# A fused macaron block: VectorE's preparation of batch 0's attention laid out anew over rounds 1 to 12 of the first feed-forward phase

## Chip, cores and metric

The kernel runs on one core of one Trainium2 chip. The metric is device time in microseconds of one execution. The five engines (TensorE, VectorE, ScalarE, GpSimd and SyncE, which issues most transfers) run programs of their own and meet at semaphores. In the profile they are PE, DVE, ACT, POOL and SP; PEld is TensorE's weight load.

## The reference, cut to what matters

`x` has 8 batches of 1024 rows of 128 float32 values.

```python
x = x + 0.5 * ffn(layernorm(x))        # FFN 1
x = x + attn(layernorm(x))             # 4 query heads, 2 key heads, causal, width 32
x = x + 0.5 * ffn(layernorm(x))        # FFN 2

def ffn(x):                            # int weights / 127, hidden 384
    return (silu(x @ wg.T) * (x @ wu.T)) @ wd.T

def attn(x):
    h = x * rsqrt(mean(x**2) + 1e-6) * norm_w
    q, k, v = h @ Wq, h @ Wk, h @ Wv
    q, k = q / |q|, k / |k|
    p = softmax(causal(q @ k.T * exp(log_temperature)))
    return x + gate * ((p @ v) @ Wo)
```

## The kernel before

All rows stay in the chip (`X`), as 16 chunks of 512 rows (4 tiles of 128). FFN 1 runs over the chunks in rounds 0 to 15, then attention runs over the 8 batches (two chunks each), then FFN 2 over the 16 chunks. Every engine's order is written out by hand: `pipeline` calls, in each round k, a list of steps with an offset to the chunk.

In round k of FFN 1:

- VectorE (`ffn_dve`): `hidden` of chunk k (silu times up, writes `H`, L327), then whatever `between[k]` holds, `stats` of chunk k+6 (L306), `residual` of chunk k-1 (L343, waits for TensorE's down product), `aggregate` of chunk k+6 (L314). Where this text says "slot k", it means the point right behind `hidden(k)`, where `between[k]` is issued.
- ScalarE (`ffn_act`): `silu(k)` (L476), four normalising activations of chunk k+3 (L458), `x_hi(k+3)` (the float16 high part of the normalised rows, L469, shown as `w_int<-XN` since it reuses that space), `h_hi(k)` (writes `HH`, L482).
- GpSimd (`ffn_pool`): `x_lo(k+3)` (the float16 low part, L426, also shown as `w_int<-XN,w_int`), `h_lo(k)` (writes `HL`, L433), and in odd rounds the row factors of two later chunks (L400 to L405, with the power at L403). Behind rounds 9 and 10 it also splits the attention input of chunks 0 and 1 in two (`AS`, L931 and L938).
- TensorE (`ffn_pe`): gate(k+1), down(k-1), up(k+1) as groups of 6 products of 512 columns (L507) and a down group that starts with L558 and goes on with `HH` and `HL` (L569). Behind rounds 11 to 14 it also does the first projections of batch 0 (L737), which wait for the weights `QKVO` (`s_wready`) and for the turned `AS` (`AXT`).
- SyncE turns each chunk's `w_int` into `XT`, and behind chunks 13 and 14 the two `AS` into `AXT`.

Batch 0's attention needs a preparation that VectorE does between these rounds: moments of chunks 0 to 3 (`stats`, L993 to L998), the weights scaled by powers of two and split into two float16 parts (`weights_scaled`, `weights_low`), a few one-column factors (`weights_factors`), the row factors of chunks 0 and 1 by an integer seed and three Newton rounds of three operations each (`factors`, i.e. `first_factors`), and the two normalised chunks (`normalise`, L1008, four operations of 128x128 each, writes `AN`). Before the change they lie in rounds 3 to 12:

```python
{3: rows("stats", 0), 4: rows("stats", 1), 5: weights_scaled,
 6: rows("factors", 0), 7: rows("factors", 1),
 8: weights_and_rows, 9: rows("normalise", 0, (2, 4)),
 10: rows("normalise", 1), 11: factors_and_rows, 12: rows("stats", 3),
```

Chunk 0 cannot be taken up by `stats` before its residual is added, which is in round 1.

Of the kernel before, what the change touches and what calls it, by code (L numbers as in the profile page):

```python
# [5 lines left out]
ALU = mybir.AluOpType  # L6
# [4 lines left out]
def macaron_kernel(nc, x, norm_w, wq, wk, wv, wo, gate, log_temp, w_gate, w_up, w_down, out):  # L11
# [38 lines left out]
    with ctx:  # L50
        def sb(name, shape, d=f32):
            return ctx.enter_context(nc.sbuf_tensor(name, shape, d))

        def sem(name):
            return ctx.enter_context(nc.semaphore(name))
# [17 lines left out]
        qkvo = sb("qkvo", [P, DQ + 2 * DK + D])  # L73
        QKVO = sb("QKVO", [P, 2, DQ + 2 * DK + D], f16)
# [5 lines left out]
        ipw = sb("ipw", [P, 4])  # L80
# [7 lines left out]
        k_lim = sb("k_lim", [P, 1])  # L88
# [30 lines left out]
        FV, FT = [sb(n, [P, 2, 2, TPC]) for n in ("FV", "FT")]  # L119
# [53 lines left out]
        a_xh0, a_fac = sem("a_xh0"), sem("a_fac")  # L173
# [808 lines left out]
        def att_dve(e, shift, first=None):  # L982
# [47 lines left out]
                e.tensor_scalar(SS[half][:, :, :], SS[half][:, :, :], 1.0 / (QSCALE * QSCALE), k_lim[:, 0:1],  # L1030
                                ALU.mult, ALU.max).then_inc(a_ss, 1)

            def root(done, n, S2, Y, T, rounds=(0, 3)):

                if rounds[0] == 0:
                    e.tensor_scalar(Y.bitcast(i32), S2.bitcast(i32), -0.5, float(0x5f3759df), ALU.mult,
                                    ALU.add).then_inc(done, 1)
                for r in range(*rounds):
                    e.wait_ge(done, n + 3 * r + 1)
                    e.scalar_tensor_tensor(T, Y, -0.5, S2, ALU.mult, ALU.mult).then_inc(done, 1)  # L1040
                    e.wait_ge(done, n + 3 * r + 2)
                    e.tensor_tensor(T, T, Y, ALU.mult).then_inc(done, 1)
                    e.wait_ge(done, n + 3 * r + 3)
                    e.scalar_tensor_tensor(Y, T, 1.5, Y, ALU.add, ALU.mult).then_inc(done, 1)
# [6 lines left out]
            def first_factors(part):  # L1051

                var, mean = AMV4[:, 0:2, :, 1], AMV4[:, 0:2, :, 0]
                V1, Y = [XP[:, 16 * i:16 * i + 16].rearrange("p (a m t) -> p a m t", a=2, m=2)
                         for i in range(2)]
                if part == 0:
                    e.wait_ge(a_stat, 4)
                    e.wait_ge(s_wtl, 3)
                    e.tensor_scalar(V1[:, 0, :, :], var, LN_EPS, None, ALU.add).then_inc(a_fac, 1)
                    e.wait_ge(a_fac, 1)  # L1060
                    e.tensor_copy(FV[:, 0, :, :], V1[:, 0, :, :])
                    e.scalar_tensor_tensor(FV[:, 1, :, :], V1[:, 0, :, :], RMS_EPS, var, ALU.mult, ALU.add)\
                        .then_inc(a_fac, 1)
                    e.wait_ge(a_fac, 2)
                    root(a_fac, 2, FV[:, :, :, :], Y, FT[:, :, :, :], (0, 1))
                    return
                root(a_fac, 2, FV[:, :, :, :], Y, FT[:, :, :, :], (1, 3))
                e.wait_ge(a_fac, 12)
                e.tensor_copy(RF4[:, :, 0:2, :], Y)
                e.tensor_scalar(A4[:, 0:2, :], Y[:, 0, :, :], 1.0, None, ALU.add)  # L1070
                e.tensor_tensor(B4[:, 0:2, :], Y[:, 0, :, :], mean, ALU.mult).then_inc(a_fac, 1)
# [305 lines left out]
        def _(e):  # L1377
            n = [0]

            def link(i):  # L1380

                n[0] += 1
                i.then_inc(s_one, 1)
                e.wait_ge(s_one, n[0])
# [54 lines left out]
            for lo, hi, c in ((0, 2 * NJ, 0), (2 * NJ, 3 * NJ, 1)):  # L1439
                i = e.scalar_tensor_tensor(w_nat[:, 1, lo:hi, :], w_flt[:, lo:hi, :], ipw[:, c:c + 1],  # L1440
                                           w_nat[:, 0, lo:hi, :], ALU.mult, ALU.subtract)
# [13 lines left out]
                link(e.tensor_copy(QKVO[:, 0, :], qkvo[:, :]))  # L1455

            def weights_low():
                e.tensor_tensor(QKVO[:, 1, :], qkvo[:, :], QKVO[:, 0, :], ALU.subtract)
                link(e.tensor_scalar(k_lim[:, :], ipw[:, 2:3], ipw[:, 2:3], None, ALU.mult))

            def weights_factors():
                e.wait_ge(s_gate_in, 16)
                e.tensor_scalar(k_wo[:, :], gate_t[:, :], pw[:, 2:3], pw[:, 3:4], ALU.mult, ALU.mult)
                e.tensor_scalar(k_lim[:, :], k_lim[:, :], (L2_MIN / QSCALE) ** 2, 1e-37, ALU.mult, ALU.max)
                e.tensor_scalar(k_exp[:, :], k_exp[:, :], 1.0 / (QSCALE * QSCALE), None, ALU.mult)\
                    .then_inc(s_wready, 1)
                e.wait_ge(s_wready, 2)

            def rows(*stage):
                return lambda: att_dve(e, False, stage)  # L1470

            def stage(name):
                return lambda: att_dve(e, False, name)

            def weights_and_rows():
                weights_low()
                rows("normalise", 0, (0, 2))()

            def factors_and_rows():
                weights_factors()  # L1480
                rows("stats", 2)()
            ffn_dve(e, 0, None, {-3: low_parts, -2: lambda: ffn_dve(e, 0, [("hidden", 0)]), NC - 1: stage("second")},
                    {3: rows("stats", 0), 4: rows("stats", 1), 5: weights_scaled,
                     6: rows("factors", 0), 7: rows("factors", 1),
                     8: weights_and_rows, 9: rows("normalise", 0, (2, 4)),
                     10: rows("normalise", 1), 11: factors_and_rows, 12: rows("stats", 3),
                     13: stage("sums"), 14: stage("unit"), 15: stage("stack")})
            stage("third")()
            hot = is_hot(e)
# [8 lines left out]
        @block.tensor  # L1498
        def _(e):
            e.wait_ge(s_const, 2)  # L1500
            e.wait_ge(s_wprep, 1)
            e.matmul(bank[0][0:4, 0, 0:P], colmax[:, 0:4], ident32[:, :], is_transpose=True,
                     start=True, stop=True)
            e.matmul(bank[0][0:1, 1, 0:P], colmax[:, 4:5], ident32[:, :], is_transpose=True,
                     start=True, stop=True).then_inc(s_wpe, 1)
            e.wait_ge(s_wprep, 2)
            e.matmul(bank[1][:, 0, 0:4], m4[:, 3:4].to_broadcast([4, P]), ident32[0:4, 0:4],
                     start=True, stop=True).then_inc(s_wpe, 1)
            e.wait_ge(s_low, 1)
            low = e.value_load(loflag[0:1, 0:1], min_val=0, max_val=1)  # L1510

            blocks = [(s, j) for s in range(2) for j in range(3 * NJ)]

            def turn_weights(parts):
                for r in parts:
                    e.wait_ge(s_wprep, 3 + min(r, 3))
                    if r == 4:
                        e.wait_ge(s_wtl, 1)
                    elif r >= 2:
                        e.wait_ge(s_wt, r - 1)  # L1520
                    dst = w_bank[r].bitcast(f16)
                    for a, (s, j) in enumerate(blocks[slice(*w_parts[r])]):
                        i = e.transpose(dst[:, a * P:(a + 1) * P], w_nat[:, s, j, :], ident16[:, :])
                    i.then_inc(s_wpe, 1)
            turn_weights((0, 1))
            hot = is_hot(e)

            def first_projection(*part):
                def project_in():
                    e.wait_ge(s_wready, 2)  # L1530
                    att_pe(e, False, part)
                return project_in

            def program(has_low):
                if has_low:
                    turn_weights((2, 3, 4))
                ffn_pe(e, 0, has_low, [("gate", 0)])
                if not has_low:
                    turn_weights((2,))
                ffn_pe(e, 0, has_low, [("up", 0)])  # L1540
                if not has_low:
                    turn_weights((3, 4))
                ffn_pe(e, 0, has_low, None, {11: first_projection(0, 0), 12: first_projection(0, 1),
                                             13: first_projection(1, 0), 14: first_projection(1, 1)})
                def head():
                    ffn_pe(e, 1, has_low, [("gate", 0)])
                def attention(e_, shift):
                    att_pe(e_, shift, None, head)
                    ffn_pe(e_, 1, has_low, None, {}, lambda: projections_read(e_, shift))
                by_heat(e, attention, hot)  # L1550
            with e.If(low < 1):
                program(0)
            with e.Else():
                program(1)
# [25 lines left out]
```

## Time and profile before

| what | value |
|---|---|
| time, median of 3 runs | 463.25 us (463.16 to 465.41) |
| the profiled execution's own time | 463.7 us |
| its span in the trace | 461.9 us |
| TensorE busy | 414.1 us, 90% |
| VectorE busy | 357.9 us, 77% |
| ScalarE busy | 383.5 us, 83% |
| GpSimd busy | 260.6 us, 56% |
| granted TensorE clock, mean | 0.999 |

The busy shares are averages over three very different phases: FFN 1 ends near 110 us of the span, and GpSimd is nearly idle in much of the attention and close to full in FFN 1. The change lies between 27 and 90 us, so that stretch has to be read by itself.

### The profile page before, as it was taken

The numbers are of one execution on the slowest core, as the hardware profiler recorded it, in microseconds if no ns is written. First come the engines' busy times: TensorE is split into PE (matmuls) and PEld (weight loads), VectorE is DVE, ScalarE is ACT, GpSimd is POOL, SyncE is SP. The second block draws the span as 40 slices with busy tenths as digits, with TensorE's granted clock in tenths as the row PEclk, the third lists the DMA queues.
The fourth block names the chain that finished last, engine by engine and source line by source line (L and its number), as shares of the span: only waits on it lengthen the run. The fifth ranks groups of instructions, "written<-read, shape, count | busy, mean of one in ns | idle before, by whom it ended". The sixth has DMA issues, their size and how long they took to land.

```text
span 461.9 us, 10471 instructions
## 1 busy us (share of the span) xinstructions
PE 414.1 (90%) x3747; PEld 214.0 (46%) x3747; DVE 357.9 (77%) x872; ACT 383.5 (83%) x546; POOL 260.6 (56%) x321
## 2 busy tenths in 40 slices
PE   0779988988998999999999999999999998999994
PEld 0346655663434435435435435335334334767654
DVE  5889998799499869869779779687556937878654
ACT  4799988875886988988988988988977998999960
POOL 5499987983625535435444444441141465999950
PEclk9999999999999999999999999999999999999999
DMA  5586521516109054065062072082070022547462
GB/s 159 130 158 148 70 46 36 103 25 125 36 4 173 10 94 91 1 112 73 0 123 58 0 135 47 1 132 53 1 138 0 16 34 47 136 92 138 92 115 73
DMA packets 119150, 34.94 MB, mean 76 GB/s; under 512 B 101568, under 2 KB 119104, under 8 KB 119104
## 3 DMA queue, kind: packets, MB, share of 16 engines
q1 hardware_dynamic: 117824, 34.02, 38.7%
q8 instruction: 26, 0.43, 0.4%
q10 hardware_dynamic: 1280, 0.33, 0.3%
q14 instruction: 20, 0.16, 0.1%
HBM read 4.98 MB, written 4.19 MB: 20 GB/s over the span
## 4 chain that ended last, share of the span: by engine, by line
PE 55%; DVE 15%; issue 12%; ACT 7%; POOL 7%; DMA 2%; DVEq 1%; SPq 0%; POOLq 0%; ACTq 0%
PE ps L507 13%; PE ps L706 11%; PE ps L687 9%; PE ps L711 9%; DVE H L327 4%; PE ps L569 4%; PE ps L558 4%; ACT PT L817 3%; PE ps L594 2%; DVE X L1021 2%; DVE AN L1008 2%; PE ps L691 2%; POOL OL L281 2%; POOL RF L925 1%; DVE bns L306 1%
## 5 line engine op out<-in xcount | busy, mean ns | idle before, releaser
L817 ACT ACTIVATE PT<-ps,k_exp 128x1024 f32<-128x1024 f32 (+1 forms) x192 | 162.1, 900 | 20.0 <-PE ps L691 14.7
L507 PE MATMUL ps<-XT,WT 128*128 128x512 f16 x384 | 95.3, 387 | 10.6 <-ACT SG L476 4.7
L687 PE MATMUL ps<-QKT 128*128 128x512 f16 (+3 forms) x384 | 87.1, 328 | 11.4 <-ACT PT L817 9.3
L706 PE MATMUL ps<-PT,V 128*32 128x512 f32 (+3 forms) x768 | 81.8, 498 | 0.0
L711 PE MATMUL ps<-PT,ones 128*32 128x512 f32 (+3 forms) x768 | 79.6, 486 | 0.0
L433 POOL TENSOR_TENSOR HL<-H,HH 128x1024 f16<-128x1024 f32 x31 | 67.2, 2167 | 10.1 <-ACT HH L482 7.9
L327 DVE SCALAR_TENSOR_TENSOR H<-SG,k_isilu,ps 128x1536 f32<-128x1536 f32 x32 | 57.8, 1807 | 14.1 <-PE ps L507 5.4
L281 POOL TENSOR_TENSOR OL<-ON,OH 128x512 f16<-128x512 f32 x15 | 18.2, 1216 | 77.3 <-ACT OH L277 77.3
L507 PEld LDWEIGHTS ps<-XT,WT 128*128 128x128 f16 x384 | 34.5, 99 | 56.2 <-issue 17.4
L687 PEld LDWEIGHTS ps<-QKT 128*128 128x128 f16 x384 | 27.8, 97 | 69.3 <-ACT PT L817 60.1
L458 ACT ACTIVATE XN<-X,NB,RS 128x128 f32<-128x128 f32 x128 | 52.4, 482 | 2.3 <-POOL NB L405 2.3
L240 DVE RECIPROCAL RD<-PVS 128x512 f32<-128x512 f32 x15 | 50.0, 3336 | 3.5 <-ACT PVS L857 3.5
L476 ACT ACTIVATE SG<-ps,k_silu 128x1536 f32<-128x1536 f32 x32 | 48.8, 1525 | 3.3 <-DVE H L327 2.2
L426 POOL TENSOR_TENSOR w_int<-XN,w_int 128x512 f16<-128x512 f32 x31 | 36.0, 1162 | 15.2 <-ACT w_int L469 15.0
L482 ACT ACTIVATE HH<-H 128x1024 f16<-128x1024 f32 x31 | 32.5, 1047 | 13.9 <-DVE H L327 13.8
L944 POOL TENSOR_TENSOR ST<-QN,ST 128x512 f16<-128x512 f32 x16 | 20.1, 1259 | 39.6 <-ACT ST L849 39.6
L711 PEld LDWEIGHTS ps<-PT,ones 128*32 128x32 f32 x768 | 24.8, 110 | 37.4 <-issue 32.4
L558 PE MATMUL ps<-WD,H 128*128 128x128 f32 x256 | 34.0, 276 | 3.6 <-DVE X L343 3.6
L558 PEld LDWEIGHTS ps<-WD,H 128*128 128x128 f32 x256 | 33.2, 191 | 8.3 <-issue 3.3
L691 PE MATMUL ps<-causal,ident 128*128 128x128 bf16 x256 | 34.3, 219 | 0.0
L343 DVE SCALAR_TENSOR_TENSOR X<-ps,k_ffn,X 128x512 f32<-128x512 f32 (+1 forms) x33 | 24.0, 728 | 13.1 <-PE ps L569 13.0
L306 DVE BATCH_NORM_STATS2 bns<-X 128x6 f32<-128x128 f32 x128 | 27.7, 278 | 5.2 <-DMA X<-in_L_attn_x 4.4
(139 smaller groups left out, 649.1 us busy)
## 6 DMA issues: line engine op xcount, KB each, us to landing
result<-X SPq DMA_DIRECT2D x15, 256.0 KB, 2.5
X<-in_L_attn_x SPq DMA_DIRECT2D x7, 512.0 KB, 4.5
X<-in_L_attn_x SPq DMA_DIRECT2D x2, 256.0 KB, 4.8
XT<-w_int SPq DMA_TRANSPOSE x32, 3.1
AXT<-AS SPq DMA_TRANSPOSE x16, 2.8
QKT<-ST SPq DMA_TRANSPOSE x16, 5.6
w_int<-in_L_ffn_w_gate SPq DMA_DIRECT2D x1, 192.0 KB, 4.0
w_int<-in_L_ffn_w_up SPq DMA_DIRECT2D x1, 192.0 KB, 4.3
```

What stands on the lines that cost most here:

```text
L240: e.reciprocal(RD[:, :], PVS[:, 1, :]).then_inc(a_rd, 1)
L327: e.scalar_tensor_tensor(H[k % 2][:, :, :], SG[:, :, :], k_isilu[:, 0:1], U, ALU.mult, ALU.mult).then_inc(s_h, 1)
L433: e.tensor_tensor(HL[k % 2][:, :], hidden_16(k), HH[k % 2][:, :], ALU.subtract)\
L458: i = e.activation(XN[k % 2][:, t, :], tile(c, t), ACT.Identity, bias=NB[:, c, t:t + 1], scale=RS[:, c, t:t + 1])
L476: e.activation(SG[:, :, :], G, ACT.Silu, scale=k_silu[:, 0:1]).then_inc(s_silu, 1)
L507: i = e.matmul(out[:, j, :], WT[:, wp, w * NJ + j, :], XT[k % 2][:, xp, :], start=a == 0, stop=a == len(passes) - 1)
L558: e.matmul(dn[:, t, :], H[k % 2][:, j, t * P:(t + 1) * P], WD[:, j, :], start=n == 0, stop=False, skip_group_check=True)
L687: i_ = e.matmul(o, QKT[k % 2][:, i // TPC, NH + hp, i % TPC * P:(i % TPC + 1) * P], QKT[k % 2][:, qc, 2 * hp + h, CH - n:CH], start=True, ...
L691: i_ = e.matmul(SCORES[hp][:, h, 0:P], ident16[:, :], causal[:, :], start=False, stop=True, skip_group_check=True)
L706: e.matmul(PVD[HD * h:HD * h + HD, 0, CH - n:CH], V[k % 2][:, i, v0:v0 + HD], PT[g % 2][:, h, 0:n], start=i == 0, stop=done, skip_group_ch ...
L711: i_ = e.matmul(PVD[HD * h:HD * h + HD, 1, CH - n:CH], ones32[:, :], PT[g % 2][:, h, 0:n], start=i == 0, stop=done, skip_group_check=True)
L817: e.activation(PT[g % 2][:, 2 * hp:2 * hp + 2, 0:n], SCORES[hp][:, :, 0:n], ACT.Exp, scale=k_exp[:, 0:1]).then_inc(a_exp, 1)
```

## The change

The table that places VectorE's pieces in rounds 1 to 12 is replaced, and two helpers are cut so that their pieces can be placed apart. The amount of arithmetic stays as it was. `root` gets a flag for its seed, `first_factors` now has four portions (seed, then one Newton round in each of three), the one-column operation on `k_lim` moves from `weights_low` to `weights_factors`, and the TensorE wait for the weights counts one signal more.

```diff
-            def root(done, n, S2, Y, T, rounds=(0, 3)):
+            def root(done, n, S2, Y, T, rounds=(0, 3), seed=True):
 
-                if rounds[0] == 0:
+                if rounds[0] == 0 and seed:
...
-                    root(a_fac, 2, FV[:, :, :, :], Y, FT[:, :, :, :], (0, 1))
+                    root(a_fac, 2, FV[:, :, :, :], Y, FT[:, :, :, :], (0, 0))
                     return
-                root(a_fac, 2, FV[:, :, :, :], Y, FT[:, :, :, :], (1, 3))
+                root(a_fac, 2, FV[:, :, :, :], Y, FT[:, :, :, :], (part - 1, part), False)
+                if part < 3:
+                    return
...
             def weights_low():
-                e.tensor_tensor(QKVO[:, 1, :], qkvo[:, :], QKVO[:, 0, :], ALU.subtract)
-                link(e.tensor_scalar(k_lim[:, :], ipw[:, 2:3], ipw[:, 2:3], None, ALU.mult))
+                i = e.tensor_tensor(QKVO[:, 1, :], qkvo[:, :], QKVO[:, 0, :], ALU.subtract)
+                i.then_inc(s_wready, 1)
 
             def weights_factors():
                 e.wait_ge(s_gate_in, 16)
+                link(e.tensor_scalar(k_lim[:, :], ipw[:, 2:3], ipw[:, 2:3], None, ALU.mult))
...
             def weights_and_rows():
+                rows("normalise", 1)()
                 weights_low()
-                rows("normalise", 0, (0, 2))()
-
-            def factors_and_rows():
+
+            def factors_and_weights():
+                rows("factors", 1)()
                 weights_factors()
-                rows("stats", 2)()
...
+                    {1: weights_scaled, 2: rows("stats", 0), 3: rows("stats", 1), 4: rows("factors", 0),
+                     5: factors_and_weights, 6: rows("factors", 2), 7: rows("factors", 3),
+                     8: rows("normalise", 0, (0, 2)), 9: rows("normalise", 0, (2, 4)),
+                     10: weights_and_rows, 11: rows("stats", 2), 12: rows("stats", 3),
...
-                    e.wait_ge(s_wready, 2)
+                    e.wait_ge(s_wready, 3)
```

The rows below are VectorE's instructions in program order, with the semaphores that they wait for. `H` is the hidden chunk, `bns` and `MV` the moments of FFN 1's chunk, `qkvo` and `QKVO` the attention weights in float32 and float16, `abns` and `AMV` the moments of batch 0's chunks.

VectorE around round 1 (chunk 1's `hidden` stands first) before the change:

```order
L327 SCALAR_TENSOR_TENSOR H<-SG,k_isilu,ps 128x1536 [waits s_up,s_silu]
L306 BN_STATS bns<-X 128x6 [waits s_stat,s_xin4]
L306 BN_STATS bns<-X 128x6 x3
L343 SCALAR_TENSOR_TENSOR X<-ps,k_ffn,X 128x512 [waits s_dn]
L314 BN_AGGR MV<-bns 128x2 [waits s_stat]
L314 BN_AGGR MV<-bns 128x2 x3
```

The same place in the changed kernel:

```order
L327 SCALAR_TENSOR_TENSOR H<-SG,k_isilu,ps 128x1536 [waits s_up,s_silu]
L1455 TENSOR_SCALAR qkvo<-qkvo,ipw 128x256 [waits s_hot]
L1456 TENSOR_SCALAR qkvo<-qkvo,ipw 128x128
L1457 CAST QKVO<-qkvo 128x384 [waits s_one]
L306 BN_STATS bns<-X 128x6 [waits s_stat,s_xin4,s_one]
L306 BN_STATS bns<-X 128x6 x3
L343 SCALAR_TENSOR_TENSOR X<-ps,k_ffn,X 128x512 [waits s_dn]
```

The three weight operations now stand ahead of round 1's moments and residual; they stood in round 5.

VectorE around round 8 before the change, where the low part of the weights stands ahead of the first two tiles of `AN`:

```order
L327 SCALAR_TENSOR_TENSOR H<-SG,k_isilu,ps 128x1536 [waits s_dn,s_up,s_silu]
L1458 TENSOR_TENSOR QKVO<-qkvo,QKVO 128x384
L1459 TENSOR_SCALAR k_lim<-ipw 128x1
L1008 TENSOR_SCALAR AN<-X,AMV,RF 128x128 [waits a_fac,s_one]
L1008 TENSOR_SCALAR AN<-X,AMV,RF 128x128
L306 BN_STATS bns<-X 128x6 [waits s_stat,s_xin8]
```

Round 8 in the changed kernel:

```order
L327 SCALAR_TENSOR_TENSOR H<-SG,k_isilu,ps 128x1536 [waits s_dn,s_up,s_silu]
L1008 TENSOR_SCALAR AN<-X,AMV,RF 128x128 [waits a_fac]
L1008 TENSOR_SCALAR AN<-X,AMV,RF 128x128
L306 BN_STATS bns<-X 128x6 [waits s_stat,s_xin8]
L306 BN_STATS bns<-X 128x6 x3
```

The two tiles now follow `hidden` directly, with nothing in front of them.

VectorE around round 10 in the changed kernel, where the low part of the weights now stands, behind chunk 1's four tiles (before, L343 followed those tiles directly):

```order
L327 SCALAR_TENSOR_TENSOR H<-SG,k_isilu,ps 128x1536 [waits s_dn,s_up,s_silu]
L1008 TENSOR_SCALAR AN<-X,AMV,RF 128x128 [waits a_fac]
L1008 TENSOR_SCALAR AN<-X,AMV,RF 128x128 x3
L1460 TENSOR_TENSOR QKVO<-qkvo,QKVO 128x384
L343 SCALAR_TENSOR_TENSOR X<-ps,k_ffn,X 128x512 [waits s_dn]
```

The other engines' programs keep their instructions and their order.

## Rows read from the trace of the kernel before

**Rows 1.** Busy time of each engine in a stretch: us (instructions); last clock, DMA share, GB/s.

```profile
28.90:47.20 18.30, 18.12 (x145) 11.87 (x144) 16.17 (x59) 18.18 (x29) 17.83 (x19) 1.00 0.67 138
```

**Rows 2.** Timeline of PE: start us, us, engine, line, operation, count [idle before <-releaser].

```profile
28.90 1.05 PE L558 MATMUL ps<-WD,H 128*128 128x128 f32 x8
...
47.21 1.05 PE L558 MATMUL ps<-WD,H 128*128 128x128 f32 x8
...
68.51 1.13 PE L558 MATMUL ps<-WD,H 128*128 128x128 f32 x8 [1.49 <-DVE X L343]
...
78.88 1.05 PE L558 MATMUL ps<-WD,H 128*128 128x128 f32 x8
...
81.12 0.62 PE L569 MATMUL ps<-WT,HL 128*128 128x128 f16 x8 [0.74 <-POOL HL L433]
```

**Rows 3.** Timeline of DVE, rounds 1 to 4.

```profile
29.23 0.86 DVE L306 BATCH_NORM_STATS2 bns<-X 128x6 f32<-128x128 f32 x4
30.88 0.75 DVE L343 SCALAR_TENSOR_TENSOR X<-ps,k_ffn,X 128x512 f32<-128x512 f32 x1 [0.79 <-PE ps L569]
...
32.23 1.81 DVE L327 SCALAR_TENSOR_TENSOR H<-SG,k_isilu,ps 128x1536 f32<-128x1536 f32 x1 [0.31 <-ACT SG L476]
...
36.81 1.81 DVE L327 SCALAR_TENSOR_TENSOR H<-SG,k_isilu,ps 128x1536 f32<-128x1536 f32 x1 [0.31 <-ACT SG L476]
38.54 0.86 DVE L993 BATCH_NORM_STATS2 abns<-X 128x6 f32<-128x128 f32 x4
...
39.74 0.84 DVE L306 BATCH_NORM_STATS2 bns<-X 128x6 f32<-128x128 f32 x4
...
41.43 1.78 DVE L327 SCALAR_TENSOR_TENSOR H<-SG,k_isilu,ps 128x1536 f32<-128x1536 f32 x1
```

**Rows 4.** Timeline of DVE: pieces of rounds 5, 7 and 11.

```profile
47.72 0.35 DVE L1453 TENSOR_SCALAR qkvo<-qkvo,ipw 128x256 f32<-128x256 f32 x1
...
48.30 1.20 DVE L1455 CAST QKVO<-qkvo 128x384 f16<-128x384 f32 x1
...
57.92 0.17 DVE L1040 SCALAR_TENSOR_TENSOR FT<-ps,FV 128x16 f32<-128x16 f32 x1
...
79.37 0.27 DVE L1463 TENSOR_SCALAR k_wo<-gate_t,pw 128x1 f32<-128x1 f32 x1
...
79.79 0.87 DVE L993 BATCH_NORM_STATS2 abns<-X 128x6 f32<-128x128 f32 x4
```

**Rows 5.** Timeline of DVE: low weights and `AN`, rounds 8 to 10.

```profile
62.82 0.55 DVE L1458 TENSOR_TENSOR QKVO<-qkvo,QKVO 128x384 f16<-128x384 f32 x1
...
63.53 1.31 DVE L1008 TENSOR_SCALAR AN<-X,AMV,RF 128x128 f32<-128x128 f32 x1
...
64.76 2.17 DVE L1008 TENSOR_SCALAR AN<-X,AMV,RF 128x128 f32<-128x128 f32 x1
...
70.27 0.59 DVE L1008 TENSOR_SCALAR AN<-X,AMV,RF 128x128 f32<-128x128 f32 x2
...
74.63 1.11 DVE L1008 TENSOR_SCALAR AN<-X,AMV,RF 128x128 f32<-128x128 f32 x4
```

**Rows 6.** Timeline of POOL.

```profile
30.27 1.16 POOL L426 TENSOR_TENSOR w_int<-XN,w_int 128x512 f16<-128x512 f32 x1
...
48.05 1.23 POOL L426 TENSOR_TENSOR w_int<-XN,w_int 128x512 f16<-128x512 f32 x1 [0.25 <-ACT w_int L469]
...
63.60 1.16 POOL L426 TENSOR_TENSOR w_int<-XN,w_int 128x512 f16<-128x512 f32 x1
64.71 2.14 POOL L433 TENSOR_TENSOR HL<-H,HH 128x1024 f16<-128x1024 f32 x1
...
71.52 2.13 POOL L433 TENSOR_TENSOR HL<-H,HH 128x1024 f16<-128x1024 f32 x1 [2.66 <-ACT HH L482]
...
74.04 1.74 POOL L403 TENSOR_TENSOR RS<-RS,nhalf 128x8 f32<-128x8 f32 x1
```

**Rows 7.** Timeline of ACT: `x_hi` of chunk 8.

```profile
47.34 0.63 ACT L469 ACTIVATE w_int<-XN 128x512 f16<-128x512 f32 x1
```

More of the change, by code:

```diff
@@ L1475, in weights_and_rows @@
             def weights_and_rows():
+                rows("normalise", 1)()
                 weights_low()
-                rows("normalise", 0, (0, 2))()
-            def factors_and_rows():
+            def factors_and_weights():
+                rows("factors", 1)()
                 weights_factors()
-                rows("stats", 2)()
             ffn_dve(e, 0, None, {-3: low_parts, -2: lambda: ffn_dve(e, 0, [("hidden", 0)]), NC - 1: stage("second")},
[L1483 to L1486, printed above, removed]
+                    {1: weights_scaled, 2: rows("stats", 0), 3: rows("stats", 1), 4: rows("factors", 0),
+                     5: factors_and_weights, 6: rows("factors", 2), 7: rows("factors", 3),
+                     8: rows("normalise", 0, (0, 2)), 9: rows("normalise", 0, (2, 4)),
+                     10: weights_and_rows, 11: rows("stats", 2), 12: rows("stats", 3),
                      13: stage("sums"), 14: stage("unit"), 15: stage("stack")})
```

## The prediction

> **What bounds the kernel now.** I first read how full each engine is in the stretch where nothing is disturbed. Over four rounds of FFN 1, 28.90 to 47.20 us, TensorE is busy 18.12 and ScalarE 18.18 of 18.30 us, GpSimd 17.83 and VectorE 16.17 [rows 1]. The down groups start at 28.90 and, four rounds later, at 47.21 [rows 2]: the pace is 18.31 / 4 = 4.58 us a round, set by TensorE and ScalarE together. With both full, a round in which VectorE is late is never won back.
>
> TensorE's timeline then shows where the pace is lost. From 47.21 to 68.51 (four rounds) it takes 21.30 us in place of 18.31, and in front of the group at 68.51 it sat idle 1.49 us for VectorE's residual; the next two rounds, to 78.88, take 10.37 in place of 9.15 [rows 2]. Together 31.67 - 6 x 4.58 = 4.2 us. That is the most that VectorE's layout can give back there.
>
> VectorE's timeline names the rounds. From `hidden(3)` at 36.81 to `hidden(4)` at 41.43 it has no gap, 4.62 us, of which the extra statistics take 39.74 - 38.54 = 1.20 [rows 3]. So a round costs it 3.42 us plus its extra piece, and the piece may take 4.58 - 3.42 = 1.16 us before the pace suffers. Before the change three kinds of piece overrun. In round 5 the scaling begins at 47.72 and its cast at 48.30 lasts 1.20 [rows 4], about 1.8 in all: 0.65 over. The two `factors` portions of rounds 6 and 7 have seven and nine operations of about 0.17 [rows 4] with a wait of some 0.04 behind most: about 1.5 each, 0.3 over each. One Newton round is three of them, 0.6. In round 8 the low weights start at 62.82 and the second tile ends at 64.76 + 2.17 = 66.93 [rows 5]: 4.1, so 2.9 over. These sum to 4.2, as TensorE's loss does.
>
> The cause in round 8 stands in the durations. A tile of `AN` costs 0.59 / 2 when nothing is in its way; here the first takes 1.31 and ends at 64.84, 0.08 behind GpSimd's `x_lo` (63.60 + 1.16 = 64.76), and the second takes 2.17 and ends 0.08 behind GpSimd's `h_lo` (64.71 + 2.14 = 66.85) [rows 5, 6]. The cast of round 5 likewise ends at 49.50, just behind `x_lo` of 48.05 + 1.23 [rows 4, 6]. So these VectorE operations wait for a GpSimd operation that is under way. They don't wait for GpSimd's power: four tiles in round 10 take 1.11 us from 74.63, inside the power of 74.04 to 75.78 [rows 5, 6].
>
> **The change, part by part.** I take the slot behind `hidden(k)` as clock: slot 3 is at 38.54 [rows 3]; at pace slot 8 is at 38.54 + 5 x 4.58 = 61.4 and slot 10 at 70.6. Before, they were at 62.82 and 74.63 [rows 5]. If each round keeps the pace, slot 10 comes 4.0 us earlier.
>
> - Round 1 gets the scaling. Start to cast is 48.30 - 47.72 = 0.58; the cast unhindered is at least the 0.22 from the end of `x_lo` (49.28) to its own (49.50), say 0.3 [rows 4, 6]. Sum 0.9, from 29.23, where slot 1 is now [rows 3], to 30.1. GpSimd's `x_lo` starts at 30.27 [rows 6], so the cast gets by, by 0.1 to 0.2. The cover is idle time of 0.79 ahead of the residual and 0.31 ahead of `hidden(2)` [rows 3], 1.10 together: cost nothing. If the cast is caught it ends about 31.5: 1.3 more, of which 0.2 is covered, 1.1 lost.
> - Rounds 2 and 3 get the statistics, 1.20: 4.62 against 4.58, nothing. What they need (residuals 0 and 1) was added a round earlier.
> - Round 4 gets the seed portion: about 1.5 less one Newton round of 0.6, 0.9. Within 1.16.
> - Round 5: one Newton round 0.6, the three one-column operations 79.79 - 79.37 = 0.42 [rows 4] and `k_lim` with its wait, an estimate of 0.24 from an operation of that size (0.27 is the largest there). Sum 1.26: 0.1 over, at most.
> - Rounds 6 and 7: 0.6, and 0.6 plus the last three operations, about 0.9. Within.
> - Round 8: two tiles, 0.59 if nothing is in their way. Before, `x_lo` came 63.60 - 62.82 = 0.78 behind the slot; the tiles now take the first 0.59 of it, so even at the old phase they are through. At pace the slot is 1.4 earlier and `x_lo` at most 1.0 earlier (GpSimd is nearly full [rows 1] and holds its own queue), so the margin grows. Saved: 2.9.
> - Round 9: slot at 66.0. `x_lo(12)` cannot begin before ScalarE's `x_hi(12)` is done: 47.34 + 0.63 + 4 x 4.58 = 66.3 [rows 7]. The two tiles end near 66.6; the second may be caught and wait the 1.16 of `x_lo`. It is cheap, as the next part shows.
> - Round 10: four tiles 1.11, low weights 0.55 [rows 5], but no statistics any more; the residual there follows at once and is needed by TensorE later. Nothing for VectorE. But GpSimd's power took 1.74 and ended at 75.78 with the last tile [rows 5, 6], so VectorE can hold back its end; another 0.5 us of VectorE behind the tiles may hold it by 0 to 0.5. I take 0.2.
>
> **What is late next.** GpSimd. From `h_lo(9)` on its queue is full in both kernels: factors, the split of `AS`, `x_lo(13)`, `h_lo(10)`, and TensorE already waits 0.74 us for the last of them [rows 2]. Before, `h_lo(9)` starts at 71.52, after an idle 2.66 for ScalarE [rows 6]. After, it follows `x_lo(12)`: 66.3 + 0.1 + 1.16 = 67.5. So GpSimd's chain, which hands over to the projections and to attention, comes 4.0 us earlier, and what VectorE loses in round 9 is hidden behind it up to about 1 us. Taken off: 0.2 for round 10, 0.1 for round 5. **Sum: 4.0 - 0.3 = 3.7 to 3.9, I take 3.8.** Everything behind round 12 has its old order and follows this chain, so the shift goes to the end: 463.7 - 3.8 = 459.9 on the profiled execution's own time. That execution is 0.45 above the median of 463.25, which gives 459.45; I say 459.5.
>
> A page's rule speaks against the free passage in round 8. The Trainium skill (SBUF — State Buffer, "SBUF: two separate sides") says that the pair of ports that VectorE and GpSimd share is locked for a whole instruction, and that the loser waits until it ends. For `x_lo`, `h_lo` and the cast the trace agrees (0.08 us behind). Held to the letter, the power would lock as well; the four tiles at 1.11 us inside it say no.
>
> **Rivals.**
>
> 1. The forecast: pace kept to round 10, GpSimd's queue next. 459.5, own range 458.9 to 460.2. Chance 0.60.
> 2. The cast of round 1 is caught by `x_lo` at 30.27, since the margin is 0.1 to 0.2: 1.1 lost, 460.6. For: GpSimd was full there [rows 1] and the rows are tight. Against: 0.9 is a sum of unhindered pieces. 0.10.
> 3. The power holds tiles after all: the two of round 8 wait until its end, 0.6 to 1.2, and may then be caught by `x_lo` (1.16 more). 0.5 to 1.5 of it reaches GpSimd's chain: 460.0 to 461.0. Against: round 10 before. This is the skill's rule above. 0.06.
> 4. The tiles of round 8 meet `x_lo` and `h_lo` as before because GpSimd runs in another phase: 3.40 - 0.59 = 2.8 stays lost, and only rounds 5 to 7 (1.3) are won: 462.0. 0.10.
> 5. GpSimd is not the next bound: the 0.74 goes too and all 4.2 comes back: about 458.3. 0.05.
> 6. The shift is given back later, in VectorE's busy stretch before attention, where its operations meet GpSimd's in another phase: within 1 us of 463.25. Against: both engines shift alike. 0.04.
> 7. Slower: tiles are caught in rounds 8, 9 and 10 alike. Two tiles behind `x_lo` and `h_lo` cost 2.8 each time, four behind four GpSimd operations about 4: 9.6 on 459.5, less 1 hidden, is 468. The point from which it decides is slot k falling into `x_lo` or `h_lo`, not the power; it would take a phase 1 us or more off in each of the three rounds. 0.05.
>
> **Numbers.** Half a per cent, 2.3 us, is about what a measurement of this kernel tells from no change; faster means below 460.9. Rivals 1, 2, 5 and most of 3 are faster: 0.80. Rivals 4, 6 and the rest of 3: 0.15. Rival 7: 0.05. Cases 1, 2, 3 and part of 4 and 5 fill 458.6 to 461.6.
>
> **What the profile of the changed kernel would show.** Right: `hidden` starts every 4.6 us from round 1 to 10; two `AN` of 0.59 in round 8 while GpSimd runs the power; slot 10 near 70.6; `h_lo(9)` near 67.5; TensorE waits for `HL` once, 0.7 to 1.1 us, behind round 10; the cast of round 1 near 0.3. Wrong: an `AN` of over 1 us in round 8 (rivals 3, 4), a cast of 1.2 or more in round 1 (rival 2), no wait for `HL` (rival 5), or a slot 10 at 70.6 and the end less than 3 us earlier (rival 6).

## The result and the profile after

The changed kernel takes 459.28 us (median of 4 executions, 459.08 to 459.96), the kernel before in the same comparison 463.31 us (463.16 to 465.41). The ratio of their times is 0.9897, 95% interval 0.9871 to 0.9924: faster by about 4.0 us by the medians and by 4.8 us by the ratio, where I had forecast 3.8. Taken by the ratio the changed kernel would stand at 458.5 us, 1.0 below the forecast of 459.5. One execution of a later experiment (`b3_casts_on_vector`, 500.64 us at a mean clock of 0.947, its profiled one) was disturbed and is left out below.

The head of the changed kernel's page. The profiled execution's own time is 459.42 us.

```profile
span 457.6 us, 10470 instructions
## 1 busy us (share of the span) xinstructions
PE 413.5 (90%) x3747; PEld 214.1 (47%) x3747; DVE 354.2 (77%) x872; ACT 382.8 (84%) x546; POOL 260.6 (57%) x321
```

The work is the same. VectorE's busy time fell by 3.7 us from 357.9, the other engines' by 0.7 at most. The 3.7 us are waiting that the trace had counted as busy: the two tiles of round 8 went from 3.40 to 0.60 and the cast from 1.20 to 0.36, 3.6 together.

TensorE's timeline after, to be read against [rows 2] (start, length, idle time before and what ended it):

```profile
28.78 1.05 PE L558 MATMUL ps<-WD,H 128*128 128x128 f32 x8
...
47.19 1.05 PE L558 MATMUL ps<-WD,H 128*128 128x128 f32 x8
...
74.64 1.05 PE L558 MATMUL ps<-WD,H 128*128 128x128 f32 x8
...
77.24 0.62 PE L569 MATMUL ps<-WT,HL 128*128 128x128 f16 x8 [1.10 <-POOL HL L433]
```

Ten rounds from 28.78 to 74.64 are 45.86 us, 4.59 each: the pace holds through round 10, and the only wait above 0.2 us is the forecast one for GpSimd's `HL`, 1.10 us. The group that stood at 78.88 stands at 74.64.

VectorE's timeline after, against [rows 4, 5]:

```profile
29.69 0.36 DVE L1457 CAST QKVO<-qkvo 128x384 f16<-128x384 f32 x1
...
61.41 0.60 DVE L1008 TENSOR_SCALAR AN<-X,AMV,RF 128x128 f32<-128x128 f32 x2
...
65.97 0.60 DVE L1008 TENSOR_SCALAR AN<-X,AMV,RF 128x128 f32<-128x128 f32 x2
...
70.55 1.11 DVE L1008 TENSOR_SCALAR AN<-X,AMV,RF 128x128 f32<-128x128 f32 x4
71.58 0.55 DVE L1460 TENSOR_TENSOR QKVO<-qkvo,QKVO 128x384 f16<-128x384 f32 x1
```

GpSimd's timeline after, against [rows 6]:

```profile
28.89 1.20 POOL L403 TENSOR_TENSOR RS<-RS,nhalf 128x4 f32<-128x4 f32 x1
30.16 0.20 POOL L405 TENSOR_TENSOR NB<-NB,RS 128x4 f32<-128x4 f32 x1
30.32 1.16 POOL L426 TENSOR_TENSOR w_int<-XN,w_int 128x512 f16<-128x512 f32 x1
...
60.82 1.64 POOL L403 TENSOR_TENSOR RS<-RS,nhalf 128x8 f32<-128x8 f32 x1
62.54 0.20 POOL L405 TENSOR_TENSOR NB<-NB,RS 128x8 f32<-128x8 f32 x1
62.70 1.16 POOL L426 TENSOR_TENSOR w_int<-XN,w_int 128x512 f16<-128x512 f32 x1
...
66.33 1.26 POOL L426 TENSOR_TENSOR w_int<-XN,w_int 128x512 f16<-128x512 f32 x1 [0.39 <-ACT w_int L469]
67.56 2.13 POOL L433 TENSOR_TENSOR HL<-H,HH 128x1024 f16<-128x1024 f32 x1
...
70.08 1.64 POOL L403 TENSOR_TENSOR RS<-RS,nhalf 128x8 f32<-128x8 f32 x1
71.79 0.40 POOL L405 TENSOR_TENSOR NB<-NB,RS 128x8 f32<-128x8 f32 x1
```

In round 8 the two tiles (61.41 to 62.01) lie inside the power (60.82 to 62.46) and end 0.69 us before `x_lo` starts at 62.70. In round 9 the second tile ends at 66.57, inside `x_lo`, and it is GpSimd that gives way: 1.26 in place of 1.16. In round 10 the low weights hold the small operation behind the power, 0.40 in place of 0.20.

### The profile page after: what moved, and what is told of

It is laid out like the page before. It is cut to its first block, busy times and chain, and to the rows that moved or that the text cites. A ratio compares the mean times of both kernels' runs of the same rounds, so it can differ in the third digit from the quotient of the medians.

```text
span 457.6 us, 10470 instructions
## 1 busy us (share of the span) xinstructions
PE 413.5 (90%) x3747; PEld 214.1 (47%) x3747; DVE 354.2 (77%) x872; ACT 382.8 (84%) x546; POOL 260.6 (57%) x321
## 4 chain that ended last, share of the span: by engine, by line
PE 51%; issue 14%; ACT 12%; DVE 11%; POOL 7%; DMA 2%; DVEq 0%; SPq 0%; POOLq 0%; ACTq 0%
PE ps L507 11%; PE ps L706 11%; PE ps L687 9%; PE ps L711 9%; ACT XN L458 4%; PE ps L558 3%; PE ps L569 3%; ACT PT L817 3%; PE ps L594 2%; DVE H L327 2%; ACT SG L476 2%; DVE X L1021 2%; PE ps L691 2%; POOL OL L281 2%; DVE AN L1008 1%
## 5 line engine op out<-in xcount | busy, mean ns | idle before, releaser
L343 DVE SCALAR_TENSOR_TENSOR X<-ps,k_ffn,X 128x512 f32<-128x512 f32 (+1 forms) x33 | 24.0, 729 | 12.2 <-PE ps L569 11.8
```

## Experiments

All are versions of one of the two kernels. Times are medians; the kernel before is timed beside each, and there came out at 464.4 to 464.7 us, over 1 us above what I had started from. That turned out to be the main finding. The traces start at different points of their execution, so where two of them are compared below, the times are counted from the start of `hidden(1)` (27.50 in the kernel before, 27.38 in the changed one).

### The low weights alone (`a1_low_moved`)

The kernel before with one part of the change.

```diff
-            def weights_and_rows():
-                weights_low()
-                rows("normalise", 0, (0, 2))()
+            def rows_and_weights():
+                rows("normalise", 1)()
+                weights_low()
...
-                     8: weights_and_rows, 9: rows("normalise", 0, (2, 4)),
-                     10: rows("normalise", 1), 11: factors_and_rows, 12: rows("stats", 3),
+                     8: rows("normalise", 0, (0, 2)), 9: rows("normalise", 0, (2, 4)),
+                     10: rows_and_weights, 11: factors_and_rows, 12: rows("stats", 3),
```

> The kernel before, with one part of the change alone: the low weights stand behind chunk 1's tiles in round 10, so that the two tiles of round 8 follow hidden(8) directly. Order theory (a tile waits for the GpSimd operation that is under way): the two tiles take 0.6 us in place of 3.40, round 8 keeps the pace, rounds 5 to 7 still lose about 1.3; slot 10 near 71.9, total about 460.5. Rival, work theory (only VectorE's surplus per round counts, the tiles of round 8 are slow for a reason of their own): only the 0.76 of the moved operation is won, about 462.5, and the tiles still take over 3 us.

Measured 460.54 us, ratio to before 0.9945 (0.9926 to 0.9965). Its seven executions lie in two groups: 460.34 to 460.54 (four) and 462.00 to 462.35 (three, the profiled one among them). VectorE and, in the second fence, GpSimd in that profiled execution:

```profile
47.33 0.42 DVE L1453 TENSOR_SCALAR qkvo<-qkvo,ipw 128x256 f32<-128x256 f32 x1
47.67 1.21 DVE L1454 TENSOR_SCALAR qkvo<-qkvo,ipw 128x128 f32<-128x128 f32 x1
48.92 2.19 DVE L1455 CAST QKVO<-qkvo 128x384 f16<-128x384 f32 x1
...
64.42 0.59 DVE L1008 TENSOR_SCALAR AN<-X,AMV,RF 128x128 f32<-128x128 f32 x2
```

```profile
47.64 1.16 POOL L426 TENSOR_TENSOR w_int<-XN,w_int 128x512 f16<-128x512 f32 x1
48.76 2.13 POOL L433 TENSOR_TENSOR HL<-H,HH 128x1024 f16<-128x1024 f32 x1
```

The tiles of round 8 are free, 0.59 against 3.40: the order theory holds and the work theory (over 3 us for the tiles, 462.5) falls. The upper group lies near its 462.5 for another reason: round 5, whose program is that of the kernel before, went otherwise than in [rows 4]. There the second scaling, at 47.99, was ahead of GpSimd's `x_lo` at 48.05, and only the cast waited, 1.20. Here the first scaling already takes 0.42 in place of 0.35 (the end of GpSimd's `h_lo(4)`, at 47.60, falls into it; that it is the cause is inferred). Then `x_lo` begins at 47.64, 0.03 before the second scaling, which takes 1.21, and the cast falls behind `h_lo` and takes 2.19. Counted from `hidden(5)` (46.03 before, 45.63 here), `x_lo` starts at 2.02 and 2.01, the second scaling at 1.96 and 2.04. So 0.08 us decides whether the scaling costs 1.8 or 3.8 us. The program is the same up to round 7, so I read this trace as the other outcome of the kernel before as well; no trace of that kernel in its upper group was taken.

### The low weights back in round 8 (`a2_low_in_8`)

```diff
-                rows("normalise", 1)()
                 weights_low()
+                rows("normalise", 0, (0, 2))()
...
-                     8: rows("normalise", 0, (0, 2)), 9: rows("normalise", 0, (2, 4)),
-                     10: weights_and_rows, 11: rows("stats", 2), 12: rows("stats", 3),
+                     8: weights_and_rows, 9: rows("normalise", 0, (2, 4)),
+                     10: rows("normalise", 1), 11: rows("stats", 2), 12: rows("stats", 3),
```

> The changed kernel, with the low weights put back ahead of the tiles in round 8. Order theory: slot 8 is at 61.4 and x_lo at 62.7, so behind 0.5 us of low weights the tiles run from 61.9 to 62.5 and still get by before x_lo; 3.42 + 0.47 + 0.59 = 4.48 stays within the pace: as the changed kernel, 459.3, with a margin of 0.2 us only. Rival (standing alone is what frees the tiles): 3.4 us for the tiles again and about 462.

Measured 459.39 us, ratio 0.9918 (0.9889 to 0.9947), as the changed kernel. VectorE in round 8:

```profile
61.23 0.55 DVE L1460 TENSOR_TENSOR QKVO<-qkvo,QKVO 128x384 f16<-128x384 f32 x1
61.70 0.60 DVE L1008 TENSOR_SCALAR AN<-X,AMV,RF 128x128 f32<-128x128 f32 x2
```

With rounds 1 to 7 laid out anew, the tiles need not stand alone: they pass in 0.60 even behind the low weights. Either half of the change frees them. What stands in front of them matters only through the time at which they start.

### Extra work ahead of and behind the tiles (`a3_work_ahead_8`, `a4_work_behind_8`)

```diff
+            def extra_work():
+                for i in range(7):
+                    e.bn_stats(extra[:, i, :], tile(0, i % TPC))
...
-                     8: rows("normalise", 0, (0, 2)), 9: rows("normalise", 0, (2, 4)),
+                     8: lambda: [extra_work(), rows("normalise", 0, (0, 2))()], 9: rows("normalise", 0, (2, 4)),
```

That is the first; the second has the two the other way round:

```diff
-                     8: rows("normalise", 0, (0, 2)), 9: rows("normalise", 0, (2, 4)),
+                     8: lambda: [rows("normalise", 0, (0, 2))(), extra_work()], 9: rows("normalise", 0, (2, 4)),
```

> The changed kernel with seven extra moment operations (1.5 us, written to a tile that nothing reads) ahead of the two tiles of round 8, which so start near 62.9, inside x_lo. Order theory: the first tile waits for x_lo (to 63.9), the second for h_lo (to 66.0); round 8 lasts about 8.0 in place of 4.58, GpSimd's h_lo(9) comes 3.1 us later, total about 462.3. Work theory: 3.42 + 1.5 + 0.6 = 5.5, 0.9 lost at most, total about 460.

> The same seven operations behind the two tiles of round 8. Both theories: tiles 0.6, round 8 5.5 us, hidden(9) 0.9 late; h_lo(9) is 0.6 later since its float16 part comes later: about 459.9. Against the run with the same work ahead this gives the price of the collision alone: 2.4 us by the order theory, 0 by the work theory.

Measured: ahead 463.49 us, ratio 0.9987 (0.9969 to 1.0004); behind 460.61 us, ratio 0.9932 (0.9910 to 0.9953). The difference is 2.9 us for the same instructions in another order, with 2.4 expected; the work theory gives 0. Up to the first products of attention the two traces differ by 2.2 us (79.03 and 76.87 behind `hidden(1)`), and this is the price of the order. The trace with the work ahead loses another 1.46 us near 150 us, in a wait for a transfer that the other doesn't have (see `b4_cast_later`), so part of the 2.9 can come from there. VectorE and then GpSimd with the work ahead:

```profile
61.70 1.45 DVE L1481 BATCH_NORM_STATS2 extra<-X 128x6 f32<-128x128 f32 x7
63.06 3.25 DVE L1009 TENSOR_SCALAR AN<-X,AMV,RF 128x128 f32<-128x128 f32 x2
```

```profile
62.99 1.16 POOL L427 TENSOR_TENSOR w_int<-XN,w_int 128x512 f16<-128x512 f32 x1
64.11 2.13 POOL L434 TENSOR_TENSOR HL<-H,HH 128x1024 f16<-128x1024 f32 x1
```

The tiles end at 66.31, 0.07 behind `h_lo`, as in [rows 5, 6]. This makes the stall of the kernel before again, by timing alone. The medians are above what was expected of each (462.3 and 459.9), by 1.2 and 0.7. With the work behind, the later slot 9 ran its first tile into `x_lo` (two tiles 1.31 in place of 0.60), which I had not foreseen. With the work ahead the ten executions spread from 462.06 to 464.76; the lowest two are where I had expected all.

### Where lateness is hidden (`b1_work_behind_10`, `b5_work_behind_6`)

The same seven operations at the end of slot 10, and behind the portion of round 6.

```diff
-                     10: weights_and_rows, 11: rows("stats", 2), 12: rows("stats", 3),
+                     10: lambda: [weights_and_rows(), extra_work()], 11: rows("stats", 2), 12: rows("stats", 3),
```

```diff
-                     5: factors_and_weights, 6: rows("factors", 2), 7: rows("factors", 3),
+                     5: factors_and_weights, 6: lambda: [rows("factors", 2)(), extra_work()], 7: rows("factors", 3),
```

> The changed kernel with seven extra moment operations (1.5 us, written to a tile that nothing reads) at the end of slot 10. Theory that GpSimd's queue is the bound there: hidden(11) comes 0.9 later, TensorE still waits about 1.1 us for HL behind down(10), nothing else moves: 459.3, as the changed kernel. Rival (VectorE still sets the time): 0.9 later, 460.2.

> The same seven operations in round 6, where by the theory TensorE and ScalarE have no slack and GpSimd follows them: round 6 lasts 3.42 + 0.6 + 1.5 = 5.5 in place of 4.58, and the 0.9 stays to the end: 460.2. Rival (GpSimd's later queue hides VectorE's lateness anywhere): 459.3.

Measured: in round 10 459.90 us (459.28 to 461.71), ratio 0.9914 (0.9883 to 0.9944); in round 6 460.97 us, ratio 0.9927 (0.9901 to 0.9954). The times spread more than the question asks (the four with the work in round 10 over 2.4 us), so the two traces have to decide, one execution each. The first products of attention come 75.78 us behind `hidden(1)` with the work in round 10, 76.45 with it in round 6, and 75.69 in the changed kernel; the spans are 457.6, 458.3 and 457.6. TensorE with the work in round 10:

```profile
76.88 0.62 PE L570 MATMUL ps<-WT,HL 128*128 128x128 f16 x8 [1.11 <-POOL HL L434]
```

The wait for `HL` is still 1.11, so GpSimd's queue is what sets the end of that stretch, and 1.4 us of VectorE there cost nothing. In round 6 it costs 0.7, where I had expected 0.9, and what round 6 lost is still there at the end: TensorE and ScalarE don't make it good. What moved the slower executions of the first version is not known.

### The scaling alone (`b2_scaling_in_1`)

The kernel before, with the scaling in round 1.

```diff
-                    {3: rows("stats", 0), 4: rows("stats", 1), 5: weights_scaled,
+                    {1: weights_scaled, 3: rows("stats", 0), 4: rows("stats", 1),
```

> The kernel before, with the scaling of the weights moved from round 5 to round 1 and nothing else. The cast takes 0.3 to 0.4, round 5 keeps the pace and wins 0.65; GpSimd and VectorE come to round 8 both 0.65 earlier, so the tiles still meet x_lo and h_lo and take 3.4: 462.6. Rival (phase has shifted enough for the tiles to get by): another 2.8 won, 459.8.

Measured 462.37 us, ratio 0.9956 (0.9936 to 0.9975). VectorE:

```profile
29.88 0.36 DVE L1455 CAST QKVO<-qkvo 128x384 f16<-128x384 f32 x1
...
62.91 3.38 DVE L1008 TENSOR_SCALAR AN<-X,AMV,RF 128x128 f32<-128x128 f32 x2
```

The tiles are still caught, as expected. What tells more is the spread: seven executions from 461.88 to 462.72, one group. The kernel before, beside it and elsewhere, has two.

### The changed kernel once more (`c3_changed_again`)

> The changed kernel once more, unedited, for the spread of its executions. Of 37 executions of the kernel before, 13 lie at 462.5 to 463.6 and the others at 464.3 to 465.5, with nothing between; with only the scaling moved to round 1 the seven executions lie in one group, 461.9 to 462.7. Theory: the scaling in round 5 is caught by one GpSimd operation or by three, by 0.1 us of phase, and that makes the two groups; the changed kernel has no such place and its executions lie in one group, 458.8 to 460.2. Rival: the two groups come from outside this place, and the changed kernel shows them too, 459.3 and 461.

Measured 459.54 us (459.30 to 459.74), ratio 0.9891 (0.9874 to 0.9907). One group, as the theory said. My count in the expectation was off: of the 37 executions before it, 15 lay at 462.5 to 463.6. With the seven of this comparison it is 16 of 44 at 462.5 to 463.6 and 27 at 464.3 to 465.5, and one, 463.97, stands between; I count it to the upper group. Of the three times that my prediction started from, two were in the lower group. The profiled execution, 463.7, is not in this count; with 463.97 it is the only one between the groups, and its round 5 went the cheap way.

### Scaling later in round 1 (`b4_cast_later`)

Three extra operations stand ahead of the scaling.

```diff
-                    {1: weights_scaled, 2: rows("stats", 0), 3: rows("stats", 1), 4: rows("factors", 0),
+                    {1: lambda: [extra_work(), weights_scaled()], 2: rows("stats", 0), 3: rows("stats", 1), 4: rows("factors", 0),
```

> The changed kernel with three extra moment operations (0.64 us, to a tile that nothing reads) ahead of the scaling in round 1, so that its cast is ready near 30.3, when GpSimd starts x_lo. Order theory: the cast waits for x_lo, takes 1.1 to 1.2 in place of 0.36, hidden(2) comes 1.2 late: about 460.5. Work theory: the extra work alone, 0.45 beyond the cover: 459.8 and a cast of 0.36.

Measured 461.26 us, ratio 0.9925 (0.9909 to 0.9942). Neither forecast fits. VectorE, GpSimd and TensorE of this run:

```profile
30.65 0.36 DVE L1458 CAST QKVO<-qkvo 128x384 f16<-128x384 f32 x1
```

```profile
29.28 1.18 POOL L404 TENSOR_TENSOR RS<-RS,nhalf 128x4 f32<-128x4 f32 x1
30.54 0.20 POOL L406 TENSOR_TENSOR NB<-NB,RS 128x4 f32<-128x4 f32 x1
30.69 1.34 POOL L427 TENSOR_TENSOR w_int<-XN,w_int 128x512 f16<-128x512 f32 x1
```

```profile
146.93 1.48 PE L738 MATMUL ps<-QKVO,AXT 128*128 128x256 f16 x12 [1.12 <-DMA AXT<-AS]
```

The cast was not caught. It began at 30.65, 0.04 ahead of `x_lo` at 30.69, and `x_lo` was the one to wait (1.34). The scaling had begun inside GpSimd's power and held its end (1.18; this size takes 1.02 in the kernel before), without which `x_lo` would have been first by about 0.1, an estimate from these lengths; the changed kernel's power is held as long (1.20). Round 1 cost 0.3 us; the first products of attention (104.07 here, 103.07 in the changed kernel's trace) come 0.6 later when counted from `hidden(1)`. The rest, 1.1 of the 1.7 us against the changed kernel's 459.54, is lost near 147 us, where TensorE waits 1.12 us for the turned `AS` of a later batch. The trace with the work ahead in round 8 has such a wait too, 1.46 us; the changed kernel's has none. The transfer is not issued later behind its input; it takes longer to land, 4.7 us or more for each of the two chunks, where in the changed kernel's trace one takes 2.8 and the other 4.5. I did not find out why.

### Two portions again (`c2_two_portions`)

```diff
             def factors_and_weights():
-                rows("factors", 1)()
                 weights_factors()
...
-                    {1: weights_scaled, 2: rows("stats", 0), 3: rows("stats", 1), 4: rows("factors", 0),
-                     5: factors_and_weights, 6: rows("factors", 2), 7: rows("factors", 3),
+                    {1: weights_scaled, 2: rows("stats", 0), 3: rows("stats", 1), 4: lambda: None,
+                     5: factors_and_weights, 6: lambda: [rows("factors", 0)(), rows("factors", 1)()], 7: lambda: [rows("factors", 2)(), rows("factors", 3)()],
```

> The changed kernel with the row factors in two portions as before (seed and one round in round 6, two rounds and the copies in round 7) and nothing of them in rounds 4 and 5. Rounds 6 and 7 then cost VectorE 4.9 each, 0.3 over the pace each: 0.6 lost, 459.9; the tiles of round 8 still get by (near 62.1 to 62.7, just ahead of x_lo). Rival: hidden behind GpSimd's queue, 459.3. A third way: the later slot 8 runs the tiles into x_lo and 461 or more follows.

Measured 459.39 us (458.96 to 460.12), ratio 0.9888 (0.9872 to 0.9905); the changed kernel in the same comparison 459.54. By the time the rival was right. In the trace its reason is not borne out: counted from `hidden(1)`, `hidden(8)` is 0.37 later than in the changed kernel, `h_lo(9)` 0.18, `h_lo(10)` 0.31 and the first products of attention 0.33, so GpSimd's queue hides little of it. The span less the start of `hidden(1)` is 430.5 us here and in the changed kernel's second trace, 430.2 in its first. Cutting the factors in four is worth at most these 0.3 us, and nothing that the times can tell.

### GpSimd's queue made shorter (`b3_casts_on_vector`, `c1_one_cast`)

The queue that is now the bound holds two casts of `AS` that VectorE could do. First both, then the first alone.

```diff
-                                  9: first(("x_hi", 0), ("x_lo", 0)), 10: first(("x_hi", 1), ("x_lo", 1)),
+                                  9: first(("x_lo", 0)), 10: first(("x_lo", 1)),
...
+            def high_part(m):
+                e.wait_ge(a_xn, m + 1)
+                e.tensor_copy(AS[m][:, 0, :, :], AN[m][:, :, :]).then_inc(a_xh0, 1)
...
             def weights_and_rows():
+                high_part(0)
                 rows("normalise", 1)()
+                high_part(1)
                 weights_low()
```

With one cast `high_part(1)` is left out, and GpSimd keeps its own for chunk 1.

> The changed kernel, with the float16 high parts of AS for chunks 0 and 1 made by VectorE in slot 10 (around chunk 1's tiles) and no longer by GpSimd. If GpSimd's queue is the bound behind round 9, its chain is 0.6 shorter up to h_lo(10) and x_lo(13): TensorE's wait for HL falls from 1.10 to about 0.5 and the end comes 0.6 earlier, 458.7. Rival (VectorE's casts hold GpSimd's power as long as they save, or another bound stands right behind): 459.3.

> The changed kernel with the float16 high part of AS for chunk 0 alone made by VectorE, first in slot 10, inside GpSimd's power. With both casts there the second one met GpSimd and took 2.25 us and the kernel was about 2 us slower than the changed one. With one: GpSimd's queue loses 0.68 ahead of h_lo(10), VectorE holds its power a little longer: TensorE's wait for HL about 0.6 in place of 1.10, end 0.4 to 0.6 earlier, 458.8. Rival: the low weights behind the tiles are now caught by the split of AS (1.16) and the residual of round 10 becomes late: 459.5 or more.

Both: 461.5 us (460.89 to 461.69 over six executions), ratio 0.9933 (0.9912 to 0.9953), 2 us above the changed kernel. Its only profile is of the execution of 500.64 us. There the second cast takes 2.25 us and ends behind `h_lo`, but the engines stand otherwise to each other than in the six, so for these it is argued, not shown. One: 458.88 us (458.75 to 459.59), ratio 0.9881 (0.9865 to 0.9897). GpSimd and TensorE with one cast:

```profile
71.61 0.66 POOL L405 TENSOR_TENSOR NB<-NB,RS 128x8 f32<-128x8 f32 x1
72.23 1.16 POOL L938 TENSOR_TENSOR AS<-AN,AS 128x512 f16<-128x512 f32 x1
```

```profile
76.67 0.62 PE L569 MATMUL ps<-WT,HL 128*128 128x128 f16 x8 [0.79 <-POOL HL L433]
```

GpSimd is spared 0.68 us. VectorE's tiles and low weights hold its small operation to 0.66 (0.40 in the changed kernel) and the power to 1.70 (1.64), so 0.36 is left. The wait for `HL` falls from 1.10 to 0.79. At 0.7 us under the changed kernel in the same comparison it is the fastest version by the medians and by the span (457.1 against 457.7), but the intervals overlap, so this is not shown.

## Why the prediction was right and where it was not

**Right: the pace and what breaks it.** TensorE kept 4.59 us a round to round 10. Slot 8 came at 61.41 (61.4 forecast), slot 9 at 65.97 (66.0), slot 10 at 70.55 (70.6). The two pairs of tiles took 0.60. That the tiles of round 8 had waited for GpSimd, and that only their start decides, is shown from both sides: by the runs with the low weights moved alone, with them put back, and with work ahead of the tiles against work behind them.

**Right: the power does not hold tiles.** Rival 3 falls: in rounds 8 and 10 they ran inside it. What [rows 5, 6] hinted at is now seen three times: VectorE holds the power's end (round 1, 1.20 in place of 1.02) or the operation behind it (round 10, 0.40 and, with one cast, 0.66 in place of 0.20).

**Right: GpSimd's queue next.** `h_lo(9)` came at 67.56 (67.5 forecast), TensorE's wait was 1.10 (0.7 to 1.1), and work added behind it in round 10 was free. The 0.2 us taken off for round 10 came out as 0.1: the low weights hold the small operation by 0.20, but the power, held by 0.10 in the kernel before, is free now. At `h_lo(9)` the shift was 3.96 us, at the first products of attention 3.91 (106.98 to 103.07), of which 0.12 was there already at `hidden(1)`: 3.79 for the stretch, against 3.8 in the sum. The profiled execution's own time came to 459.42, where the sum gave 459.9; the 0.4 us more were won behind the first products of attention, and the changed kernel's second trace has only 0.1 of them. I can't say what they are.

**Right in direction, half in size: rounds 6 and 7.** The sum gave them 0.3 each. In the trace with two portions 0.33 of the 0.6 reaches attention once the other rounds keep the pace, and the times don't tell it from nothing.

**Wrong: the term of round 5, and the baseline with it.** The step that failed is "In round 5 the scaling begins at 47.72 and its cast at 48.30 lasts 1.20 [rows 4], about 1.8 in all: 0.65 over". That was one of two outcomes, and the term was too small for the kernel as a whole. In the profiled execution GpSimd's `x_lo` started 0.06 us behind the second scaling and caught the cast alone. In the other outcome, seen in the trace of `a1_low_moved`, it catches the second scaling, `h_lo` catches the cast, and the piece takes 3.8 us, 2.6 over.

I had read the 465.41 among the three times as noise. It belongs to a group of its own, about 1.6 us above the other, in which the kernel before ran in 28 of 44 executions. With the scaling in round 1 it is gone: one group in the seven executions of `b2_scaling_in_1` and in the eight of the changed kernel. So the term should have been 0.65 or, with the 1.6 us between the groups, 2.3: some 1.7 on average, 1.0 more than I gave it.

The change is worth 3.7 us against the lower group (median 463.1, and 459.5 for the changed kernel) and 5.2 against the upper (464.7). The later comparisons, medians 464.4 to 464.7 before, give 5 us. My sum is near for the execution that I worked from, and too small for the kernel. That the median of the first comparison came within 0.3 us of 459.5, and 4.0 of 3.8, is in part luck: three of its four executions of the kernel before were in the lower group.

I had the mechanism in hand: the prediction weighs a margin of 0.1 to 0.2 us for the cast in round 1 (rival 2, 0.10) and never asks what margin the second scaling of round 5 had had. In round 1 the margin came out larger, 0.27 and 0.52 us in the two traces of the changed kernel, in part since GpSimd's power waits for VectorE and `x_lo` is pushed back with it.

By the Trainium skill (SBUF — State Buffer, "SBUF: two separate sides") the first to start gets the shared ports for its whole instruction, and on VectorE's side this concerns operations in a two-port mode or with two inputs in SBUF. The operations caught in rounds 5 and 8 agree: tiles and scalings end 0.07 to 0.08 us behind GpSimd's, casts 0.22 (the prediction put the cast at 0.08 as well, which its own figures, 49.28 and 49.50, don't give). The power disagrees, as above: tiles ran to their end inside it.

Open: why the transfer of a later batch's turned `AS` was late in two of the traces; why some versions of the changed kernel spread over 1.7 to 2.5 us (`a2_low_in_8`, `b1_work_behind_10`, `a4_work_behind_8`) with the scaling out of round 5, so that this place is not the only source of spread; and whether the second cast was caught in the version with two.

## What to carry to other kernels

Where VectorE and GpSimd share a stretch, read the start of each VectorE operation against what GpSimd is running, and give each pair its margin. A margin under 0.1 us, as in round 5, has to be taken as a coin: the profile shows one side, and the spread of the times can show that there is another. Let short, blockable operations run beneath those of GpSimd that don't block them (here the power), and before adding work to a full engine ask which later queue would hide its lateness.

## What the runs showed of the hardware

- A tile of `AN` (128x128 float32, scalars from SBUF) takes 0.33 us alone, 1.31 when it waits for a GpSimd operation of 1.16, 2.17 when it waits for one of 2.14.
- The distance between two engines varies from execution to execution: in two traces of the same changed kernel GpSimd's power of round 1 started 1.51 and 1.76 us behind `hidden(1)`. In round 5, 0.08 us between two traces separate a piece of 1.8 us from one of 3.8; the two groups of times, 1.6 us apart, are put down to this.
- The waiting is mutual: GpSimd's power of 128x4 took 1.06 to 1.20 in place of 1.02 when its end fell under VectorE's scaling or cast, `x_lo` 1.23 to 1.34 in place of 1.16, and the small product 0.40 to 0.66 in place of 0.20.
